# Cross-attention and a fake-quantized FFN on one Trainium2 core: block 1's deviations turned on TensorE, q scaled ahead of the maxima, a ring for the contraction's sums, tokens dealt four in a row, a shorter front of the expansion

## The reference

```python
x = x + xattn(layernorm(x), ctx, ctx, Wq, Wo)    # 16 heads of 32, the same Wq for Q, K and V
x = x + ffn(layernorm(x), clip_x, clip_down, w_gate, w_up, w_down)

# ffn, QMAX = 127
def act_q(x, clip):                              # one scale for the whole tensor
    scale = sigmoid(clip) * max(abs(x)) / QMAX
    return clip_(round(x / scale), -QMAX - 1, QMAX) * scale
# weights: the same with a scale of max(abs(row)) / QMAX for each row
h = act_q(silu(act_q(x) @ wq(w_gate).T) * (act_q(x) @ wq(w_up).T), clip_down)   # 1408 inner features
return h @ wq(w_down).T
```

## Time and profile before

| What | Value |
|---|---|
| median of 3 runs | 1153.25 us |
| profiled execution, its own time | 1156.43 us |
| its span on the core | 1154.6 us |
| mean granted TensorE clock | 0.979 |
| TensorE busy | 1096.4 us, 95% of the span |
| VectorE, ScalarE, POOL busy | 764.8, 619.8 and 403.0 us |
| attention | to 658.4 us |
| expansion | 658.4 to 977.2 us |
| contraction | 977.2 us to the end |
| all DMA | 223.18 MB, mean 193 GB/s; 388 to 424 GB/s in the first four of the contraction's slices |

### The profile page before, as it was taken

The page is one execution under the profiler, slowest core; times in us unless marked ns, Lnnn a source line. Parts: engine busy times, 40 slices in busy tenths (PEclk is TensorE's granted clock), DMA queues, the critical chain, the costliest instruction groups (busy, mean ns, idle before and its releaser), DMA issues. The chain is left out here.

```text
span 1154.6 us, 17335 instructions
## 1 busy us (share of the span) xinstructions
PE 1096.4 (95%) x6142; PEld 616.8 (53%) x6142; DVE 764.8 (66%) x1383; ACT 619.8 (54%) x760; POOL 403.0 (35%) x321
## 2 busy tenths in 40 slices
PE   8689999999999999999999799999999997899898
PEld 5555666666666666666665444444444443344333
DVE  6445777677767666665554667777777777675665
ACT  4246556555555546555445257565656563755350
POOL 5355444455444544444331000000000000456678
PEclk9899999999999999999999989999999999899999
DMA  6333776568655576456436446767676522999977
GB/s 238 98 52 83 189 200 181 122 187 225 162 131 141 187 183 157 112 160 146 66 109 209 142 147 239 233 233 237 233 240 225 164 33 78 388 413 417 424 286 262
DMA packets 149535, 223.18 MB, mean 193 GB/s; under 512 B 67920, under 2 KB 76752, under 8 KB 143568
## 3 DMA queue, kind: packets, MB, share of 16 engines
q1 hardware_dynamic: 149456, 222.16, 61.9%
HBM read 137.41 MB, written 72.52 MB: 182 GB/s over the span
## 5 line engine op out<-in xcount | busy, mean ns | idle before, releaser
L1052 POOL TENSOR_TENSOR c_y<-x,c_y 128x512 f32<-128x512 f32 x64 | 112.4, 1785 | 395.2 <-DVE c_y L1086 377.5
L716 PE MATMUL a_Q<-a_xT,wq 128*128 128x512 f32 x768 | 197.1, 407 | 11.0 <-DVE a_q L615 11.0
L974 PE MATMUL e_G<-e_cT,gu 128*128 128x512 bf16 x704 | 181.8, 381 | 1.1 <-ACT e_cT L897 1.1
L883 ACT ACTIVATE e_sg<-e_G,x_gus 128x512 f32<-128x512 f32 x176 | 119.0, 685 | 117.1 <-PE e_G L974 117.1
L978 PE MATMUL e_U<-e_cT,gu 128*128 128x512 bf16 x704 | 181.7, 381 | 0.0
L938 DVE SCALAR_TENSOR_TENSOR h<-e_U,x_gus,e_sg 128x512 f32<-128x512 f32 x176 | 131.8, 749 | 72.7 <-PE e_U L978 47.3
L751 PE MATMUL a_O<-a_wo,a_aT 128*128 128x512 f32 x720 | 176.5, 394 | 0.0
L716 PEld LDWEIGHTS a_Q<-a_xT,wq 128*128 128x128 f32 x768 | 142.4, 192 | 63.8 <-issue 35.8
L1124 PE MATMUL c_Y<-dn,gu 128*128 128x512 bf16 x704 | 156.6, 386 | 14.3 <-DVE gu L1079 14.3
L419 POOL TENSOR_TENSOR a_aT<-a_att,a_aT 128x512 fp32r<-128x512 f32 x64 | 82.5, 1290 | 212.1 <-ACT a_aT L492 212.1
L515 ACT ACTIVATE a_qT<-a_q 128x512 fp32r<-128x512 f32 x64 | 40.4, 632 | 208.9 <-DVE a_q L615 203.4
(11 more groups left out here) (127 smaller groups left out, 1234.5 us busy)
## 6 DMA issues: line engine op xcount, KB each, us to landing
x<-x_d SPq DMA_DIRECT2D x32, 1024.0 KB, 7.1
h_d<-h SPq DMA_DIRECT2D x24, 1024.0 KB, 4.1
h<-h_d SPq DMA_DIRECT2D x11, 1536.0 KB, 18.0
a_xr<-in_x SPq DMA_DIRECT2D x64, 256.0 KB, 3.9
a_xt<-in_xT SPq DMA_DIRECT2D x64, 256.0 KB, 4.8
x_d<-a_xr SPq DMA_DIRECT2D x64, 256.0 KB, 3.5
a_xs<-in_x SPq DMA_DIRECT2D x60, 256.0 KB, 4.8
out<-c_y SPq DMA_DIRECT2D x15, 1024.0 KB, 10.4
```

What stands on the lines that cost most here:

```text
L716: mm = nc.tensor.matmul(Q[:], wq[:, wp, j, P * n.g:P * (n.g + 1)], xT[:, n.par, xp, j], start=(ins == 0), stop=(ins == 3 * KT - 1))
L883: nc.scalar.activation(sg[:, s], G[:, t % GU], ACT.Silu, scale=gus[:, t:t + 1]).then_inc(silued, 1)
L974: mm = nc.tensor.matmul(G[:, t % GU], gu[:, t, k], cT[:, p, k], start=(k == 0), stop=(k == KT - 1))
L1052: nc.gpsimd.tensor_tensor(y[:, p, t], x1[:, p, t], y[:, p, t], ALU.add).then_inc(added, 1)
```

## The change

1. In attention, rs of block 1 no longer goes through DRAM. `turn_rs(1)` turns it on TensorE in slot 0 and VectorE copies it to `rsb` before the first q of block 1. The DRAM path starts with block 2.
2. On VectorE the scaling of q stands ahead of the reduction to maxima in each slot, no longer behind it.
3. The four stores of w_down's scale are issued in four slots, one each, and the load behind them five slots later than before.
4. Tokens are dealt: tile t holds the tokens 4p+t of a block in partition p, no longer 128t+p. x1_d is laid out [block, partition, tile, feature], so that the load of a block of x1 and the store of a block of output have 8 KB in one piece for each partition. x tiles are read and x1 tiles written with 2 KB pieces 8 KB apart. The transposed x is laid out to match on the host.
5. The expansion's front: eps is added inside ScalarE's logarithm, the Newton step has three instructions instead of four, the maximum is turned without the copy over 128 columns, 1/sigmoid(clip) is multiplied in while TensorE turns, and the factors of the first four columns come before the others and before the other scales. The turned codes are copied in four quarters, and the first matmuls wait for one quarter each.
6. The contraction: all engines unrolled. Block 0 is coded and cast in six pieces of 1, 1, 2, 2, 2 and 3 inner tiles, and TensorE runs over the inner tiles outside and the token tiles inside. x1 has four slots in a ring (two of them new, `z`), the sum is written in place over x1 and stored from there, and `y` has only two slots of one tile each between VectorE and POOL. SyncE loads x1 of block k+1 when block k-3 is stored. The later blocks' matmuls wait for the first of two pieces only. The last block's sums are VectorE's.

The core of the diff:

```diff
-    x1_d = dram("x1_d", [BLOCKS, TT, P, D], F32)
+    x1_d = dram("x1_d", [BLOCKS, P, TT, D], F32)
...
-    x_t = x.rearrange("b (n t p) d -> (b n) t p d", t=TT, p=P)
+    x_t = x.rearrange("b (n p t) d -> (b n) t p d", t=TT, p=P)
     x_k = xT_all.rearrange("(k p) (b t) -> b k p t", p=P, t=TOK)
-    out_t = out.rearrange("b (n t p) d -> (b n) t p d", t=TT, p=P)
+    out_t = out.rearrange("b (n p t) d -> (b n) p t d", t=TT, p=P)
...
-                    if k == W_FIRST + WSTEPS + 5:
-                        sp.wait_ge(w_scaled, 2 * IT + KT)
-                        for r in range(KT):
-                            sp.dma_start(dsc_d[r], dsc[:, r:r + 1]).then_inc(ds_out, 16)
-                    if k == W_FIRST + WSTEPS + 7:
+                    row = k - (W_FIRST + WSTEPS + 6)
+                    if 0 <= row < KT:
+                        sp.wait_ge(w_scaled, 2 * IT + row + 1)
+                        sp.dma_start(dsc_d[row], dsc[:, row:row + 1]).then_inc(ds_out, 16)
+                    if k == W_FIRST + WSTEPS + 12:
...
-                    if k % 4 == 2 and (n := at(k, 6)) and n.block > 0:
+                    if k % 4 == 2 and (n := at(k, 6)) and n.block > 1:
...
+                    if (n := at(k, 4)):
+                        dve.wait_ge(q_done, n.n + 1)
+                        after(dve, qT_l, n.n)
+                        if n.n == TT:
+                            dve.wait_ge(r_turned, 2)
+                            dve.wait_ge(q_scaled, TT)
+                            nc.vector.tensor_copy(rsb[:], A[:]).then_inc(rsb_rdy, 1)
+                            dve.wait_ge(rsb_rdy, 2)
+                        if n.block > 1:
+                            dve.wait_ge(rsb_in, 16 * (n.block - 1))
+                        nc.vector.tensor_tensor(q32[:], Q[:], rsb[:], ALU.mult).then_inc(q_scaled, 1)
...
-                    if (n := at(k, 4)):
-                        dve.wait_ge(q_done, n.n + 1)
-                        after(dve, qT_l, n.n)
-                        if n.block > 0:
-                            dve.wait_ge(rsb_in, 16 * n.block)
-                        nc.vector.tensor_tensor(q32[:], Q[:], rsb[:], ALU.mult).then_inc(q_scaled, 1)
...
+                def turn_rs(b):
+
+                    pe.wait_ge(rs_rdy, b + 1)
+                    after(pe, rsb_rdy, b)
+                    for t in range(TT):
+                        mm = nc.tensor.transpose(A[:, P * t:P * (t + 1)], rs[:, t:t + 1].to_broadcast([P, P]), id32[:])
+                    mm.then_inc(r_turned, 1)
...
+                    if k == 0:
+                        turn_rs(1)
...
-                nc.scalar.activation(lnv[:], ve[:], ACT.Ln).then_inc(s_aown, 1)
+                act.wait_ge(s_eps, 1)
+                nc.scalar.activation(lnv[:], var, ACT.Ln, bias=epsb[:, 0:1]).then_inc(s_aown, 1)
...
+                own.step(nc.vector.reciprocal(clip[:], sig[:, 0:1]))
 
                 dve.wait_ge(s_r0, 1)
-                own.step(nc.vector.tensor_tensor(rt[:], r0[:], r0[:], ALU.mult))
-                own.step(nc.vector.tensor_tensor(rt[:], rt[:], ve[:], ALU.mult))
-                own.step(nc.vector.tensor_scalar(rt[:], rt[:], -0.5, 1.5, ALU.mult, ALU.add))
-                own.step(nc.vector.tensor_tensor(rs[:], rt[:], r0[:], ALU.mult))
+                own.step(nc.vector.scalar_tensor_tensor(out=rt[:], in0=var, scalar=EPS, in1=r0[:], op0=ALU.add, op1=ALU.mult))
+                own.step(nc.vector.scalar_tensor_tensor(out=rt[:], in0=rt[:], scalar=-0.5, in1=r0[:], op0=ALU.mult, op1=ALU.mult))
+                own.step(nc.vector.scalar_tensor_tensor(out=rs[:], in0=rt[:], scalar=1.5, in1=r0[:], op0=ALU.add, op1=ALU.mult))
...
-                own.step(nc.vector.tensor_reduce(tmax[:], hi[:], AX.X, ALU.max))
-                nc.vector.tensor_copy(tall[:], tmax[:].to_broadcast([P, P])).then_inc(s_tmax, 1)
+                nc.vector.tensor_reduce(tmax[:], hi[:], AX.X, ALU.max).then_inc(s_tmax, 1)
+                own.step(nc.vector.tensor_scalar(rs[:], rs[:], clip[:, 0:1], QMAX, ALU.mult, ALU.mult))
...
+                own.step(nc.vector.reciprocal(inv[:], gmax[:]))
+                for a, z in ((0, TT), (TT, TILES)):
+                    own.step(nc.vector.tensor_scalar(xmul[:, a:z], rs[:, a:z], inv[:, 0:1], None, ALU.mult))
+                    nc.vector.scalar_tensor_tensor(out=xadd[:, a:z], in0=mean[:, a:z], scalar=-1.0, in1=xmul[:, a:z],
+                                                   op0=ALU.mult, op1=ALU.mult).then_inc(s_scale, 1)
...
+                                pe.wait_ge(first_odd if k % 2 else first_even, k // 2 + 1)
...
+        FIRST_CH = ((0, 1), (1, 2), (2, 4), (4, 6), (6, 8), (8, IT))
...
+        def ring(k):
+
+            return x1[:, k % 4] if k % 4 < 2 else z[:, k % 4 - 2]
...
+                load_x1(2)
+                load_x1(3)
+                for k in range(BLOCKS + 1):
...
                     if k >= 2:
-
-                        if k - 2 < BLOCKS - 1:
-                            sp.wait_ge(added, (k - 1) * TT)
-                        if k - 2 < BLOCKS - 1:
-                            sp.dma_start(out_t[ORDER[k - 2]].rearrange("t p d -> p t d"), y[:, k % 2]).then_inc(y_out[k % 2], 16)
-                        if k < BLOCKS:
-                            load_x1(k)
+                        sp.wait_ge(added, (k - 1) * TT)
+                        sp.dma_start(out_t[ORDER[k - 2]], ring(k - 2)).then_inc(y_out[(k - 2) % 4], 16)
+                    if 3 <= k < LAST:
+
+                        sp.wait_ge(y_out[(k - 3) % 4], 16 * ((k - 3) // 4 + 1))
+                        load_x1(k + 1)
...
+                for k in range(LAST):
+                    residual_in(pool, k)
                     for t in range(TT):
-                        pool.wait_ge(scaled, k * TT + t + 1)
-                        nc.gpsimd.tensor_tensor(y[:, p, t], x1[:, p, t], y[:, p, t], ALU.add).then_inc(added, 1)
-
-                add(0, 0)
-                add(0, 1)
-                with pool.Fori(1, LAST) as u:
-                    for p in range(2):
-                        add(u, p)
+                        i = k * TT + t
+                        pool.wait_ge(scaled, i + 1)
+                        nc.gpsimd.tensor_tensor(ring(k)[:, t], ring(k)[:, t], y[:, i % 2], ALU.add).then_inc(added, 1)
...
+                def scale(k):
                     for t in range(TT):
-                        dve.wait_ge(downed, k * TT + t + 1)
-                        nc.vector.tensor_tensor(y[:, p, t], Y[:, TT * p + t], dns[:], ALU.mult).then_inc(scaled, 1)
-
-                own = Chain(dve, s_own)
+                        i = k * TT + t
+                        after(dve, added, min(i - 1, LAST * TT), 1 << 30)
+                        dve.wait_ge(downed, i + 1)
+                        nc.vector.tensor_tensor(y[:, i % 2], Y[:, TT * (k % 2) + t], dns[:], ALU.mult).then_inc(scaled, 1)
+                        if k == LAST:
+                            dve.wait_ge(scaled, i + 1)
+                            if t == 0:
+                                residual_in(dve, k)
+                            nc.vector.tensor_tensor(ring(k)[:, t], ring(k)[:, t], y[:, i % 2], ALU.add).then_inc(last_added, 1)
+                            dve.wait_ge(last_added, t + 1)
...
+                for k in range(BLOCKS):
+                    if k < LAST:
+                        to_bf16(k + 1)
+                    scale(k)
...
+                for j in range(IT):
+                    pe.wait_ge(cast, upto(0, max(hi for lo, hi in FIRST_CH if lo <= j)))
+                    for t in range(TT):
+                        mm = nc.tensor.matmul(Y[:, t], cb[:, 0, j, P * t:P * (t + 1)], dn[:, :, j],
+                                              start=(j == 0), stop=(j == IT - 1))
+                        if j == IT - 1:
+                            mm.then_inc(downed, 1)
...
                     for t in range(TT):
                         after(pe, scaled, (k - 2) * TT + t + 1, 1 << 30)
                         for j in range(IT):
-                            mm = nc.tensor.matmul(Y[:, TT * p + t], cb[:, p, j, P * t:P * (t + 1)], dn[:, :, j],
+                            if t == 0:
+                                pe.wait_ge(cast, upto(k, CH[j >= CH[0][1]][1]))
+                            mm = nc.tensor.matmul(Y[:, TT * (k % 2) + t], cb[:, k % 2, j, P * t:P * (t + 1)], dn[:, :, j],
                                                   start=(j == 0), stop=(j == IT - 1))
                         mm.then_inc(downed, 1)
```

More of the change, by code:

```diff
@@ L920, in _ @@
                 own.step(nc.vector.tensor_scalar(sx[:], gmax[:], sig[:, 0:1], 1.0 / QMAX, ALU.mult, ALU.mult))
-                own.step(nc.vector.reciprocal(inv[:], sx[:]))
-                own.step(nc.vector.tensor_scalar(xmul[:], rs[:], inv[:, 0:1], None, ALU.mult))
-                own.step(nc.vector.scalar_tensor_tensor(out=xadd[:], in0=mean, scalar=-1.0, in1=xmul[:], op0=ALU.mult, op1=ALU.mult))
```

(12 more changed lines are left out.)

144 lines of the change are left out of this document (62 added, 82 removed).

## The result

The changed kernel takes 1139.51 us (median of 4 runs, 1137.92 to 1141.78); the kernel before, beside it, 1153.47 (1152.59 to 1154.49). The ratio is 0.988, with a 95% interval of 0.9861 to 0.9899. That is faster, as forecast, and inside the range of 1123 to 1141, but by 14.0 us and not by 22.3, and outside the forecast's own narrower range of 1124 to 1136. The profiled execution took 1141.78 us with a span of 1139.9, 14.65 less than the profiled one before.

| part | forecast | measured |
|---|---|---|
| attention | -5.8 | -1.1 |
| start of the expansion (with its low clock) | -1.9 | -2.1 |
| start of the contraction | -5.8 | -5.6 |
| contraction's stream of matmuls | -7.1 | -4.4 |
| tail | -1.7 | -1.5 |

What follows compares the result with a forecast made beforehand. TensorE was taken as the bound, busy 579 of 590 us in attention. Terms -5.8-1.9-5.8-7.1-1.7 = -22.3 us against the profiled 1156.43 gave 1134.1, by median 1131; range 1123 to 1141.

Steps and rivals of the forecast that it cites:

- the prediction's own sign: Attention: the account counts as wrong if attention ends less than 3 us earlier.
- the loop's sign: Contraction's loop: the account counts as wrong if TensorE idles over 6 us there.
- Block 1, -9.2: Attention, block 1: q scaled earlier and rs turned on TensorE; scoring at about 54.8 instead of 63.98, gain 9.2 us.
- The swap's price in later blocks: Attention: with q ahead of the maxima, VectorE's reduction waits whenever q waits; +2.0 us for three late blocks, ends 0 and 4.
- Block 2, +3.0: Attention, block 2: the reduction stands behind a q waiting for its row through DRAM; 2.2 us plus 0.8 for lower clock.
- Block 15, -1.6: Attention, block 15: spreading the four dscale stores removes the late landing, 1.6 us gained; ends +2.5 and -2.
- Expansion, -1.9: Start of the expansion: shorter chain to the scale, -1.2 us, and starting on a quarter of the turned codes, -0.65.
- Start of the contraction, -5.8: Contraction's start: coding and casting one tile first brings the first matmul from 985.72 to 979.9 us.
- The loop, -7.1: Contraction's stream of matmuls: 163.2 us less 6.6 of waits and 2 of lower clock, plus 1.5 for late x1: 156.1.
- The rival of VectorE and GpSimd by turns: Contraction: two-slot y makes VectorE and POOL take turns, making the kernel slower, up to 1171 us; chance 0.05.
- Tail, -1.7: Kernel's end after TensorE's last matmul: VectorE does the last sums, 4.0 us instead of 5.7.
- the swap gives attention's gain back: Attention: late rows of 1/sigma stop reductions and pull the clock down; attention +1, total 1138 us; chance 0.12.

Runs made afterwards that it cites:

- kernels with fillers: Changed kernel, q first before the fifth slot alone, plus unread TensorE work at stage borders: 1132.09 us; the second also queues x1 ahead of h: 1128.12 us.

## Why the prediction was right within its range and wrong in attention

The time lies 8.5 us above the forecast of 1131 and inside the wide range, whose upper end was set by the rivals' times. By the prediction's own sign (attention ending less than 3 us earlier) its account of attention was wrong; the loop's sign (TensorE idle under 6 us) held.

- *Block 1, -9.2*: right in the trace (-9.9), 3 of it by the swap. With the old order, and with block 15's 1.6 among it, it is worth 5.4 us to the end.
- *The swap's price in later blocks*: **this step failed**, and in two places. "A wait of w costs about w less 1, so some 0.5 and 1.5 in two of them: +2.0" took the six waits of before as given. But q asks for its row earlier now, while the row comes no earlier: in blocks 3 to 14 it lands 6.6 us (median) behind the start of scoring in the slot that needs it, in both kernels, as SyncE issues its load only when the row's stores have landed. So q waits in 13 blocks. Blocks 3 to 14 cost 8.6 us (from -6.4 at slot 5 to +2.2 at slot 26), not 2.0; 2.9 of it fall at slot 8 by way of w_inv and the exponential. And "rs is itself ready about 0.5 earlier" was wrong in sign: its store starts 10.1 us behind the start of scoring in slot 2 where it was 7.5. Of the 2.6, 1.5 are slot 2 itself, part of it at the lower clock, and 1.1 the chain, which I priced at its durations of before without asking what GpSimd does in its new place. The right order was the old one in every slot: undoing the swap gives the 6.7 us back.
- *Block 2, +3.0*: about right (3.5 from slot 2 to slot 5). *Block 15, -1.6*: right.
- *Expansion, -1.9*: right in sum (-2.1), in part by luck: the chain and the copy gave 1.2 of it in this pair of profiles and the clock the rest. The profile of the experiment that undoes it shows 2.0 for chain and copy.
- *Start of the contraction, -5.8*: right (-5.6).
- *The loop, -7.1*: right in kind, with late x1 mis-sized. I allowed 1.5 us for it and expected it in blocks 9 to 12 with the queue at 11.6 us a block; it cost 3.1 in the profiled run (blocks 7 to 11, 11.7 us a block), 3.5 to 4.6 in kernels without fillers whose attention ends earlier. Block 0 took 12.56 us, 2.9 above the 9.70 at full clock, where 2.1 were allowed. The 1.6 and 0.8, with 0.3 of rest, are the 2.7 by which the stream is longer than forecast. The rival of VectorE and GpSimd by turns is out: with the loads thinned out, no wait is left. One figure under the 156.1 was wrong: 38.16 us for 176 matmuls are 0.2168 each and not 0.2157, 152.6 for 704, so the surplus over them was 10.6 and not 11.4. In the changed kernels 660 matmuls without a pause took 142.61, 0.2161 each.
- *Tail, -1.7*: right (-1.5). But the tail before was long because x1 was late for the last block; with the old contraction and x1 less late it is 4.6 us, only 0.4 more than the new one.
- The rival "the swap gives attention's gain back" (attention +1, chance 0.12) is closest to what attention did (-1.1). It was thought of and priced, and put low because O's projection would cover the waits. It covers most of the 13, but TensorE's waits in blocks 2, 5 and 7 (5.13, 2.42 and 0.81 us) are enough, together with a granted clock of 0.50 from 78.3 and from 197.8 us, at the first two of them.

## What to carry to other kernels

Before an operation is moved ahead of another on an engine's queue, ask what it waits for at its new time, not at its old one: a wait that was hidden behind the other operation becomes the other operation's wait. Price small operations at the place where they will run, with what GpSimd does there. And where a stage is bound by full queues, a gain ahead of it is partly handed back, until the order of the transfers follows the order in which they are wanted.

## What the runs showed of the hardware

- A 128x4 VectorE operation with two SBUF inputs takes 0.16 us alone and 1.22 beside a 128x512 subtraction on GpSimd: it ends with that one. A 128x4 tensor_scalar goes from 0.17 to 0.52 beside a cast of 0.61 us, and to 0.45 beside a 128x308 operation of 1.06.
- One core moves 422 GB/s for 110 us on end in the contraction (985 to 1095 us of the changed kernel), and 426 for 50 us with x1 ahead of h, reads and stores of device memory together.
- The granted clock at the two borders of stages is 0.50, over windows of 10 and 6 us, when TensorE pauses there in pieces of 2.2 to 5.1 us, and 1.00 when transpositions and matmuls fill those pauses, down to rests of 1.5 us and less. Both kernels with fillers show it.
- A row of 128x4 numbers goes through device memory in 4-byte pieces and back as a broadcast. The load is issued 8.5 to 15.4 us behind the first store (this includes SyncE's own order; the medians of the kernels are 9.9 to 11.1) and takes 5.5 to 7.1 us (medians) to land.
